# An f32 FFN kernel on one core: a weight's high half moved to VectorE, a small conditioning network moved between convolutions

## The chip, the cores and the metric

One Trainium2 chip, one of its cores. The metric is the time on the device, in microseconds, of one execution of the whole program. The time before is the median of three runs.

## What is computed

`x` is 32 samples of 32 channels by 512 positions. Two layers follow one another, each with a residual. Cut to what matters here:

```
h   = conv1d(x, K=9, 4 groups) + (cond_128 @ c_weight.T)[:, :, None] + bias
h2  = relu(h @ up_w)**2 @ down_w
h3  = ((h @ fc1_w) @ expert_w) * (sum of the top two of h @ gate_w) @ fc2_w
x   = x + layernorm(h2 + h3)

a   = gelu(cond_128 @ W0 + b0); a = gelu(a @ W1 + b1)
att = softmax(a @ W2 + b2)                 # 32 samples x 8 kernels
agg_w = einsum('bk,koi->boi', att, weight); agg_b = att @ bias_k
y   = agg_w @ x + agg_b                    # a 32x32 mixing of channels, per sample
x   = x + y @ W.T + b + (attention over eight low-rank adapters of y)
```

The "conditioning network" of the title is the lines for `a`, `att`, `agg_w` and `agg_b`. It needs only `cond_128` and weights, and its results are first read by the mixing of the second layer.

## The kernel before, in words

The order of the work on every engine is written out by hand: one function per engine, with semaphores between them. Each engine takes its instructions strictly as they are written, so an instruction that waits holds up everything behind it on that engine.

A tile is four samples (128 rows of X). There are eight tiles, taken in two halves of four (`HALVES`, `TPH`). Products with f32 weights are made of three f32r products, since each operand is split into a high and a low part (`mm3`, L1212 to L1216: high by high, high by low, low by high). The high part is a cast, the low part a subtraction; ScalarE mostly makes the first, VectorE or GpSimd the second.

**The opening.** TensorE convolves the four tiles of the first half (L1233), turns the expert weight (L1396), makes the context rows (L1428) and adds them to the convolutions (`conv_bias`, L1246, which waits for the context rows `s_rows`). Then it multiplies expert and fc2 weights once for all ("E2", L1430 to L1439), for which fc2 must be split: ScalarE casts the high half (L713, L714, into a part of `dn_lo`), GpSimd then subtracts (L555, L556). VectorE in this stretch makes the context rows in four small steps (L985 to L993), the low half of the turned expert weight (L997), two pieces of the up weight's low half (`split_up`, L864) and the four tiles of the activation's low half (`split_H`, L885). TensorE's first `up` chunk waits for the last of these.

**A half.** For each of eight chunks c of the inner dimension TensorE runs `up(c)` (12 matmuls), ScalarE takes the relu, VectorE squares it, both split it into `R_hi`, `R_lo`, and TensorE runs `down(c)` (12 matmuls) into the four banks D. Behind up(0) it runs `gate_rows` (8 matmuls), behind up(1) `gate_logits` (four transposes of 16 rows), behind up(2) two `latent` chunks, and `routed` behind down(1).

**The conditioning network, before.** In the first half TensorE's loop calls `conditioning(c)` (L1459 and following) behind down(2) to down(6): first layer (L1464), second layer (L1467), logits (L1470), transposition of the attention weights (`turn_att`, L1443) and `mixing` (bias L1451, weights L1456). ScalarE takes `hidden` (gelu, L738) and `exp_att` (L743) in c = 5 to 7, VectorE `att_scores` and `att_weights` (L1019 to L1031) in c = 7. The second half begins with VectorE's `split_attT`, `copy_aggb` and `turn_agg` (L1040 to L1051).

**Between the halves.** TensorE runs the four convolutions of the second half back to back (`conv(4)` to `conv(7)`, 24 passes each), then down(7) of the first half, then up(8), the first up chunk of the second half. Per tile VectorE adds the context (`add_ctx`, L874), ScalarE casts (`split_H`, L667), VectorE subtracts (`split_H`, L890). up(8) waits for all four. Then VectorE takes `norm_stats` and `norm_apply` of the first half's tiles (L948 to L965) between the steps of up(8) and up(9).

The matrix banks are D (4), U (2) and M (2). A convolution of the second half writes U[0], U[1], M[0], M[1] in turn (`conv_bank`). The name `fc` in rows of the trace is the buffer `fc2`; once fc2 is split, `cond` is laid over it and holds the network's weights and small results. The buffer shown as `attT` is `attT3` or `attT2`, `tf` a staging buffer, `dn_lo` also fc2's halves, `ex_lo` also the turned expert weight.

```
            for h in range(HALVES):
                if h:
                    conv(TPH)
                    for t in range(1, TPH):
                        conv(TPH + t)
                    down(IC - 1)
```

Of the kernel before, what the change touches and what calls it, by code (L numbers as in the profile page):

```python
# [12 lines left out]
P = 128  # L13
# [3 lines left out]
def bass_adaln_ffn(  # L17
# [89 lines left out]
    with ExitStack() as ctx:  # L107
# [10 lines left out]
        QK = [(U[0], U[1]), (M[0], M[1])]  # L118
        wc_bank = (M[1], U[1], D[1])
# [103 lines left out]
        h1, h2 = cond[:, 288:288 + N], cond[:, 320:320 + N]  # L223
# [406 lines left out]
        def _(act):  # L630
# [82 lines left out]
            act.wait_ge(ld_fc2, 16)  # L713
            nc.scalar.activation(fc2_hi, fc2[:], ACT.Copy).then_inc(s_fc2h, 1)  # L714
# [20 lines left out]
            def hidden(i):  # L735

                act.wait_ge((s_c1p, s_c2p)[i], 1)
                nc.scalar.activation((h1, h2)[i], M[0][:, 0:N], ACT.Gelu, bias=(b0, b1)[i])\  # L738
                    .then_inc((s_c1, s_c2)[i], 1)
# [10 lines left out]
            def copy_attT():  # L750
                act.wait_ge(s_aTp, 1)
                nc.scalar.activation(attT3[:], M[0][0:96, 0:N], ACT.Copy).then_inc(s_aT, 1)
                nc.scalar.activation(attT2[:], M[0][0:KE, 0:N], ACT.Copy).then_inc(s_aT, 1)

            for h in range(HALVES):
                i0 = h * IC
                if h:
                    for t in range(TPH):
                        split_H(TPH + t)
# [22 lines left out]
                for c in range(3, IC):  # L782
                    if h == 0:
                        split_dn(c)
                        if c in (5, 6):
                            hidden(c - 5)
                        if c == 7:
                            exp_att()
# [7 lines left out]
                    if h == 0 and c == IC - 1:  # L796
                        copy_attT()
# [54 lines left out]
        def _(dve):  # L852
# [129 lines left out]

            dve.wait_ge(ld_fs, 16)
# [33 lines left out]
            def att_scores():  # L1017
                dve.wait_ge(s_lgp, 1)
                nc.vector.tensor_tensor(att[:, 0, :], M[0][0:N, 0:KE], b2, ALU.add).then_inc(s_att, 1)  # L1019
# [18 lines left out]
            def split_attT():  # L1038
                dve.wait_ge(s_aT, 1)
                nc.vector.tensor_tensor(attT3[64:96], M[0][64:96, 0:N], attT3[64:96].bitcast(F32),  # L1040
                                        ALU.subtract).then_inc(s_aTl, 1)

            def copy_aggb():
                dve.wait_ge(s_aggbp, 1)
                nc.vector.tensor_copy(aggb[:], U[1][0:N, 0:C]).then_inc(s_aggb, 1)

            def turn_agg():

                dve.wait_ge(s_AGp, 1)
                for b in range(2):  # L1050
                    nc.vector.transpose(agg[:, b * (C // 2):(b + 1) * (C // 2), :].rearrange("i o n -> i (o n)"),  # L1051
                                        M[b][0:C, :]).then_inc(s_agg, 1)

            for h in range(HALVES):
                i0 = h * IC
                if h:
                    split_attT()
                    copy_aggb()
                    turn_agg()
                    for T in range(TPH, TILES):  # L1060
                        add_ctx(T)
                        split_H(T)
                    norm_stats(0)
                    norm_stats(1)
                    norm_apply(0)
# [15 lines left out]
                if h:  # L1081
                    norm_apply(2)
# [10 lines left out]
                for c in range(3, IC):  # L1093
                    if h == 0 and c == 7:
                        att_scores()
                        att_weights()
# [114 lines left out]
        def _(pe):  # L1211
# [6 lines left out]
            def conv(T, samples=range(SPT)):  # L1218
# [42 lines left out]
            def gate_logits(h):  # L1261

                pe.wait_ge(s_gTs, h + 1)
                if h:
                    pe.wait_ge(s_tf, TPH)
# [5 lines left out]
            def up(i):  # L1271
# [4 lines left out]
                if c < 2:  # L1276
                    pe.wait_ge(s_H, TPH * (h + 1))
                    if h:
                        pe.wait_ge(s_tf, c + 1)
# [21 lines left out]
            def down(i):  # L1301
# [5 lines left out]
                for t in range(TPH):  # L1307
                    if h and c == 0:
                        pe.wait_ge(s_x1, t + 1)
                    if h == 0 and c == 0:  # L1310
# [129 lines left out]

            def turn_att():
                pe.wait_ge(s_att, 5)
                nc.tensor.transpose(M[0][0:96, 0:N], att3[:].rearrange("n b k -> n (b k)"), ident[0:N, 0:N])\  # L1443
                    .then_inc(s_aTp, 1)

            def mixing():

                pe.wait_ge(s_aT, 2)
                pe.wait_ge(s_aTl, 1)
                pe.wait_ge(s_R, IC)  # L1450
                nc.tensor.matmul(U[1][0:N, 0:C], attT2[:], bk[:],  # L1451
                                 start=True, stop=True).then_inc(s_aggbp, 1)
                pe.wait_ge(s_wk, 1)
# [109 lines left out]
```

## Time and profile before

| | |
|---|---|
| median of 3 runs | 217.27 us (217.12 to 217.29) |
| the profiled execution, its own time | 217.51 us |
| its span in the trace | 215.7 us |
| TensorE busy | 211.2 us, 98% of the span |
| VectorE busy | 124.8 us, 58% |
| ScalarE busy | 80.1 us, 37% |
| GpSimd busy | 61.8 us, 29% |
| granted TensorE clock | 1.0 of full speed in all slices |

The span is what the trace covers; 1.8 us of the execution's time lie around it. A busy share says how long an engine had an instruction in it, not that the work was dense. The chain of waits follows the work that ended last back to its start, and gives for each matmul the time until the next one could go, so an instruction that makes its neighbour late shows there as a longer piece.

### The profile page before, as it was taken

The numbers are of one execution on the slowest core, as the hardware profiler recorded it, in microseconds if no ns is written. First come the engines' busy times: TensorE is split into PE (matmuls) and PEld (weight loads), VectorE is DVE, ScalarE is ACT, GpSimd is POOL, SyncE is SP. The second block draws the span as 40 slices with busy tenths as digits, with TensorE's granted clock in tenths as the row PEclk, the third lists the DMA queues.
The fourth block names the chain that finished last, engine by engine and source line by source line (L and its number), as shares of the span: only waits on it lengthen the run. The fifth ranks groups of instructions, "written<-read, shape, count | busy, mean of one in ns | idle before, by whom it ended". The sixth has DMA issues, their size and how long they took to land.

```text
span 215.7 us, 3106 instructions
## 1 busy us (share of the span) xinstructions
PE 211.2 (98%) x1155; PEld 183.4 (85%) x1155; DVE 124.8 (58%) x265; ACT 80.1 (37%) x156; POOL 61.8 (29%) x77
## 2 busy tenths in 40 slices
PE   7999899999999999999999999999999999999994
PEld 7997778888887789987888888888998998999984
DVE  4979356869525455597852034456996537435443
ACT  5998555369384612222222034431013112121110
POOL 3018421340475620021960012442264202202000
PEclk9999999999999999999999999999999999999999
DMA  6999655310000000174645000000000110110104
GB/s 177 346 406 406 219 116 109 61 27 0 0 3 0 0 0 3 25 123 68 91 41 146 0 0 0 3 0 2 0 3 0 49 49 3 50 49 0 52 0 146
DMA packets 31455, 14.94 MB, mean 69 GB/s; under 512 B 25336, under 2 KB 26168, under 8 KB 31440
## 3 DMA queue, kind: packets, MB, share of 16 engines
q1 hardware_dynamic: 30624, 14.05, 23.4%
q10 hardware_dynamic: 816, 0.69, 1.5%
q8 instruction: 9, 0.15, 0.3%
q14 instruction: 6, 0.05, 0.1%
HBM read 12.62 MB, written 2.11 MB: 68 GB/s over the span
## 4 chain that ended last, share of the span: by engine, by line
PE 95%; DVE 4%; issue 0%; DVEq 0%
PE PS L1214 26%; PE PS L1216 25%; PE PS L1215 25%; PE PS L1233 9%; PE PS L1341 3%; PE PS L1403 2%; DVE up_lo L864 1%; DVE H_lo L885 1%; PE PS L1258 1%; PE PS L1257 1%; PE PS L1412 1%; PE PS L1370 0%; PE PS L1267 0%; DVE ex_lo L997 0%; DVE up_hi L993 0%; PE PS L1456 0%
## 5 line engine op out<-in xcount | busy, mean ns | idle before, releaser
L910 DVE TENSOR_TENSOR PS<-PS,relu 128x512 f32<-128x512 f32 x16 | 11.2, 699 | 30.9 <-ACT relu L675 30.9
L1214 PE MATMUL PS<-H_hi,up_hi 128*128 128x512 f32 x64 | 25.6, 399 | 0.5 <-DVE H_lo L885 0.5
L1216 PE MATMUL PS<-H_hi,up_lo 128*128 128x512 f32 x64 | 25.0, 390 | 0.0
L1215 PE MATMUL PS<-H_lo,up_hi 128*128 128x512 f32 x64 | 25.0, 390 | 0.0
L1233 PE MATMUL PS<-wconv,XS 128*128 128x128 f32 x192 | 22.4, 276 | 0.0
L1233 PEld LDWEIGHTS PS<-wconv,XS 128*128 128x128 f32 x192 | 21.9, 192 | 0.3
L1216 PE MATMUL PS<-qkT_hi,H_lo 128*128 128x320 f32 x64 | 19.8, 309 | 0.0
L1215 PE MATMUL PS<-qkT_lo,H_hi 128*128 128x320 f32 x64 | 19.8, 309 | 0.0
L1214 PE MATMUL PS<-qkT_hi,H_hi 128*128 128x320 f32 x64 | 19.7, 308 | 0.0
L675 ACT ACTIVATE relu<-PS 128x512 f32<-128x512 f32 x16 | 9.5, 594 | 25.5 <-PE PS L1216 23.0
L595 POOL TENSOR_TENSOR X<-X,rowb 128x512 f32<-128x512 f32 x8 | 10.3, 1297 | 28.1 <-PE PS L1341 28.1
L1214 PE MATMUL PS<-dn_hi,ring 128*128 128x512 f32 x44 | 17.4, 396 | 0.0
L1216 PE MATMUL PS<-dn_hi,ring 128*128 128x512 f32 x44 | 17.2, 390 | 0.0
L1215 PE MATMUL PS<-dn_lo,ring 128*128 128x512 f32 x44 | 17.1, 389 | 0.0
L567 POOL TENSOR_TENSOR dn_lo<-dn_raw,dn_hi 128x512 fp32r<-128x512 f32 x8 | 10.3, 1291 | 22.2 <-ACT dn_hi L655 22.2
L449 ACT ACTIVATE XS<-X 32x128 f32<-32x128 f32 (+2 forms) x24 | 15.8, 658 | 0.4
L448 DVE COPY XS<-X 32x128 f32<-32x128 f32 (+2 forms) x40 | 15.2, 380 | 0.7
L1214 PEld LDWEIGHTS PS<-H_hi,up_hi 128*128 128x128 f32 x64 | 12.0, 188 | 3.4 <-issue 0.9
L1216 PEld LDWEIGHTS PS<-H_hi,up_lo 128*128 128x128 f32 x64 | 12.0, 188 | 2.6
L1215 PEld LDWEIGHTS PS<-H_lo,up_hi 128*128 128x128 f32 x64 | 12.0, 188 | 2.3
L1214 PE MATMUL PS<-wT_hi,H_hi 128*128 128x512 f32 (+1 forms) x36 | 13.7, 381 | 0.0
L1216 PE MATMUL PS<-wT_hi,H_lo 128*128 128x512 f32 (+1 forms) x36 | 13.2, 367 | 0.0
(187 smaller groups left out, 459.6 us busy)
## 6 DMA issues: line engine op xcount, KB each, us to landing
up_raw<-in_L_ffn_up_w_dram SPq DMA_DIRECT2D x2, 1024.0 KB, 8.9
dn_raw<-in_L_ffn_down_w_dram SPq DMA_DIRECT2D x2, 1024.0 KB, 13.0
out_dram<-X SPq DMA_DIRECT2D x7, 256.0 KB, 2.0
X<-in_x_dram SPq DMA_DIRECT2D x1, 1024.0 KB, 13.9
XS<-in_L_ffn_W_dram SPq DMA_DIRECT2D x16, 64.0 KB, 2.3
X<-in_x_dram SPq DMA_DIRECT2D x2, 256.0 KB, 2.9
X<-in_x_dram SPq DMA_DIRECT2D x1, 512.0 KB, 5.4
fc<-in_L_ffn_fc_w_dram SPq DMA_DIRECT2D x1, 512.0 KB, 5.7
```

Of the source, the lines that this page charges most:

```text
L448: return nc.vector.tensor_copy(dst, src)
L449: return nc.scalar.activation(dst, src, ACT.Copy)
L567: nc.gpsimd.tensor_tensor(dn_lo[:, c, :], dn_raw[:, c, :], dn_hi[:, c, :].bitcast(F32), ALU.subtract).then_inc(s_dn, 1)
L595: nc.gpsimd.tensor_tensor(X[:, T, :], X[:, T, :], rowb[:], ALU.add).then_inc(s_x1b, 1)
L675: nc.scalar.activation(relu[:], U[i % 2], ACT.Relu).then_inc(s_relu, 1)
L910: nc.vector.tensor_tensor(U[i % 2], U[i % 2], relu[:], ALU.mult).then_inc(s_sq, 1)
L1214: nc.tensor.matmul(o, lh, rh, start=start, stop=False)
L1215: nc.tensor.matmul(o, lh, rl, start=False, stop=False)
L1216: return nc.tensor.matmul(o, ll, rh, start=False, stop=stop)
L1233: last = nc.tensor.matmul(conv_bank(T)[:, s * P:(s + 1) * P], XS[:, T % TPH * SPT + s, a:a + P], wconv[:, a], start=(a == 0 and (T >= TPH ...
L1341: last = nc.tensor.matmul(mix_bank(T)[:, p, :], X[:, T, p * P:(p + 1) * P], BD[:, T], start=True, stop=True)
L1403: nc.tensor.matmul(D[0][:, 0:w], ones[:], ones[:, 0:w], start=True, stop=True)
```

## The change

- **Opening.** The cast of fc2's high half leaves ScalarE. VectorE makes it behind `cT` and `cwT` and ahead of the context rows.
- **The network's matrix steps** leave the first half's loop. The first layer goes ahead of conv(4), the second behind it, the logits behind conv(5), the transposition behind conv(7). Three of them now take or give full 128-column operands (`h2_wide`, `att3_wide`, `ident[:]`).
- **Mixing** goes behind up(8), and its bias product, now `mixing_bias`, behind the second half's `gate_logits`. Banks change accordingly (`agg_bank` is M[1], U[1]; logits M[1]; transposition U[0]; bias D[0]).
- **ScalarE** takes gelu, gelu, exp and the two small copies in turn ahead of the four casts of the second half's tiles. **VectorE** takes the softmax steps behind tile 5, `split_attT` ahead of tile 7's subtraction, `turn_agg` between `norm_stats(1)` and `norm_apply(0)`, `copy_aggb` behind the ninth chunk's split.
- Waits follow: conv(6) waits for the second gelu, conv(7) for the first softmax step, up(9) for both halves of `turn_agg`, up(8) for the turned weights beside the tiles; gate_logits of the second half waits for one half of `turn_agg`.

```diff
@@ scalar @@
             for i in range(3):
                 shift_copies(i)
-            act.wait_ge(ld_fc2, 16)
-            nc.scalar.activation(fc2_hi, fc2[:], ACT.Copy).then_inc(s_fc2h, 1)
             act.wait_ge(s_exTp, 1)
...
                 if h:
-                    for t in range(TPH):
-                        split_H(TPH + t)
+                    hidden(0)
+                    split_H(TPH)
+                    hidden(1)
+                    split_H(TPH + 1)
+                    exp_att()
+                    split_H(TPH + 2)
+                    copy_attT()
+                    split_H(TPH + 3)
                 up_relu(i0)
@@ vector @@
             nc.vector.tensor_copy(cwT[:], M[0][:, N:N + C]).then_inc(s_cT, 1)
 
+            dve.wait_ge(ld_fc2, 16)
+            nc.vector.tensor_copy(fc2_hi, fc2[:]).then_inc(s_fc2h, 1)
             dve.wait_ge(ld_fs, 16)
...
                 if h:
-                    split_attT()
-                    copy_aggb()
-                    turn_agg()
                     for T in range(TPH, TILES):
                         add_ctx(T)
+                        if T == TILES - 1:
+                            split_attT()
                         split_H(T)
+                        if T == TPH + 1:
+                            att_scores()
+                            att_weights()
                     norm_stats(0)
                     norm_stats(1)
+                    turn_agg()
                     norm_apply(0)
...
                 up_split(i0 + 1)
                 if h:
+                    copy_aggb()
                     norm_apply(2)
@@ tensor @@
                 if T == TPH:
                     pe.wait_ge(s_R, IC)
-                if T == TPH + 1:
-                    pe.wait_ge(s_aggb, 1)
                 if T == TPH + 2:
-                    pe.wait_ge(s_lat, LC)
-                    pe.wait_ge(s_agg, 2)
+                    pe.wait_ge(s_c2, 1)
+                if T == TPH + 3:
+                    pe.wait_ge(s_att, 1)
...
+                    if h and c == 0:
+                        pe.wait_ge(s_tf, 1)
+                        pe.wait_ge(s_aT, 2)
+                        pe.wait_ge(s_aTl, 1)
+                    elif h:
+                        pe.wait_ge(s_agg, 2)
...
+            def cond_logits():
+                pe.wait_ge(s_c2, 1)
+                nc.tensor.matmul(M[1][:, 0:KE], h2_wide, W2, start=True, stop=True).then_inc(s_lgp, 1)
+
             def turn_att():
                 pe.wait_ge(s_att, 5)
-                nc.tensor.transpose(M[0][0:96, 0:N], att3[:].rearrange("n b k -> n (b k)"), ident[0:N, 0:N])\
-                    .then_inc(s_aTp, 1)
+                pe.wait_ge(s_tf, 1)
+                nc.tensor.transpose(U[0][:, 0:P], att3_wide, ident[:]).then_inc(s_aTp, 1)
...
                 if h:
+                    cond_layer0()
                     conv(TPH)
-                    for t in range(1, TPH):
-                        conv(TPH + t)
+                    cond_layer1()
+                    conv(TPH + 1)
+                    cond_logits()
+                    conv(TPH + 2)
+                    conv(TPH + 3)
+                    turn_att()
                     down(IC - 1)
 
                 up(h * IC)
+                if h:
+                    mixing()
                 gate_rows(h)
                 up(h * IC + 1)
                 gate_logits(h)
+                if h:
+                    mixing_bias()
                 up(h * IC + 2)
```

TensorE where the halves meet, before: bias and weights of the mixing, then all 48 convolution matmuls, in one piece.

```order
L1216 MATMUL PS<-dn_hi,ring 128x512
L1451 MATMUL PS<-bk,attT 32x32
L1456 MATMUL PS<-lat_hi,attT 32x512 x2
L1233 MATMUL PS<-wconv,XS 128x128 x48
L1214 MATMUL PS<-dn_hi,ring 128x512
```

And with the change (L1451 is now the first layer, L1455 the second, L1459 the logits, L1464 the transposition):

```order
L1219 MATMUL PS<-dn_hi,ring 128x512
L1451 MATMUL PS<-cT,fc 128x32
L1235 MATMUL PS<-wconv,XS 128x128 x12
L1455 MATMUL PS<-fc 128x32
L1235 MATMUL PS<-wconv,XS 128x128 x12
L1459 MATMUL PS<-fc 128x8
L1235 MATMUL PS<-wconv,XS 128x128 x24
L1464 MATMUL PS<-ident,fc 128x128
```

The convolutions are cut in three places, and the mixing has left this stretch for the one behind up(8).

VectorE in the opening, with the change. The row L984 is new; the rows around it stand in the order that they had.

```order
L981 COPY cwT<-PS 128x32
L984 CAST dn_lo<-fc 128x1024
L987 TENSOR_TENSOR rows<-PS,fsb 64x32
L989 CAST rows_hl<-rows 64x32
L991 TENSOR_TENSOR rows_hl<-rows,rows_hl 32x32
L995 TENSOR_TENSOR up_hi<-rows_hl,turn 64x512
L999 TENSOR_TENSOR ex_lo<-PS,ex_lo 128x512
L864 TENSOR_TENSOR up_lo<-up_raw,up_hi 128x512 x2
L885 TENSOR_TENSOR H_lo<-PS,H_hi 128x4x128 x4
```

The cast now stands ahead of the four small steps of the context rows, which `conv_bias` waits for.

VectorE between the halves, with the change, from tile 5's subtraction to tile 7's:

```order
L890 TENSOR_TENSOR H_lo<-tf,H_hi 128x4x128
L1021 TENSOR_TENSOR fc<-PS,fc 32x8
L1023 TENSOR_REDUCE fc<-fc 32x1
L1025 TENSOR_SCALAR fc<-fc 32x8
L1030 RECIPROCAL fc<-fc 32x1
L1033 TENSOR_SCALAR fc<-fc 32x3x8
L874 TENSOR_TENSOR tf<-PS,B 128x4x4x32
L890 TENSOR_TENSOR H_lo<-tf,H_hi 128x4x128
L874 TENSOR_TENSOR tf<-PS,B 128x4x4x32
L1042 TENSOR_TENSOR attT<-PS,attT 32x32
L890 TENSOR_TENSOR H_lo<-tf,H_hi 128x4x128
```

Five softmax steps and one subtraction are new between the tiles' steps.

## Rows read from the trace of the kernel before

**Rows 1.** The page's chain that ended last, by engine.

```profile
PE 95%; DVE 4%; issue 0%; DVEq 0%
```

**Rows 2.** Waits of TensorE in total, times, longest (us).

```profile
PE PS L1214 <- DVE H_lo L885: 0.5, 1, 0.5
```

**Rows 3.** Chain in order of time, opening: start us, us, what.

```profile
14.82 0.16 PE PS L1428 x2
...
15.50 0.19 DVE rows_hl L989
...
15.71 0.68 DVE up_hi L993
...
17.08 2.71 DVE up_lo L864 x2
19.79 2.41 DVE H_lo L885 x4
...
22.33 0.47 PE PS L1214
```

**Rows 4.** Line L864: duration ns min/median/max, first and last start.

```profile
L864 DVE TENSOR_TENSOR up_lo<-up_raw,up_hi x8: 680/682/2185, 17.0 to 57.6; 128x512 fp32r<-128x512 f32 x8
```

**Rows 5.** Timeline, opening, three engines: start us, us, engine, line, what [idle before].

```profile
13.60 0.18 DVE L981 COPY cwT<-PS 128x32 f32<-128x32 f32 x1
...
14.81 1.06 ACT L714 ACTIVATE dn_lo<-fc 128x1024 fp32r<-128x1024 f32 x1
...
16.02 2.62 POOL L556 TENSOR_TENSOR dn_lo<-fc,dn_lo 128x1024 fp32r<-128x1024 f32 x1 [2.08 <-ACT dn_lo L714]
...
23.45 2.40 POOL L563 TENSOR_TENSOR fc_lo<-fc_raw,fc_hi 128x1024 fp32r<-128x1024 f32 x1 [2.45 <-ACT fc_hi L731]
...
17.48 1.19 PE L1246 MATMUL PS<-up_hi,ones_r 128*128 128x512 f32 x4
```

**Rows 6.** Groups of VectorE by form: busy us, mean ns | idle before.

```profile
L448 DVE COPY XS<-X 32x512 f32<-32x512 f32 x10 | 6.1, 607 | 0.1
...
L1036 DVE TENSOR_TENSOR lat_hi<-tf,lat_hi 32x1024 fp32r<-32x1024 f32 x1 | 1.2, 1215 | 0.2 <-ACT lat_hi L748 0.2
```

**Rows 7.** Chain in order of time, TensorE in the first half's loop.

```profile
57.66 0.14 PE PS L1464 x2
57.80 0.31 PE PS L1214
...
69.08 0.16 PE PS L1470 x2
69.24 0.43 PE PS L1214
```

**Rows 8.** Chain in order of time, TensorE where the halves meet.

```profile
78.02 0.17 PE PS L1451 x2
78.19 0.59 PE PS L1456 x2
78.78 10.72 PE PS L1233 x96
```

**Rows 9.** Timeline between the halves, VectorE and ScalarE.

```profile
81.50 0.69 DVE L874 TENSOR_TENSOR tf<-PS,B 128x512 f32<-128x512 f32 x1 [1.38 <-PE PS L1233]
...
90.92 0.69 DVE L890 TENSOR_TENSOR H_lo<-tf,H_hi 128x512 fp32r<-128x512 f32 x1 [0.70 <-ACT H_hi L667]
...
72.22 1.28 ACT L743 ACT_TABLE_LOAD   x1
```

**Rows 10.** Timeline and chain, up(8) to up(10): VectorE, then TensorE.

```profile
78.82 1.30 DVE L1051 STREAM_TRANSPOSE qk_raw<-PS 32x512 f32<-32x512 f32 x2 [0.41 <-PE PS L1456]
...
97.87 0.68 DVE L914 TENSOR_TENSOR ring_last<-PS,ring_last 128x512 fp32r<-128x512 f32 x1
...
99.52 0.35 PE PS L1267 x4
99.86 0.43 PE PS L1214
```

More of the change, by code:

```diff
@@ L118, in bass_adaln_ffn @@
         QK = [(U[0], U[1]), (M[0], M[1])]
+        agg_bank = (M[1], U[1])
         wc_bank = (M[1], U[1], D[1])
@@ L222, in bass_adaln_ffn @@
         b0, b1, b2 = cond[:, 264:265], cond[:, 265:266], cond[0:N, 266:266 + KE]
-        h1, h2 = cond[:, 288:288 + N], cond[:, 320:320 + N]
+        h1, h2, h2_wide = cond[:, 288:288 + N], cond[:, 0:N], cond[:, 0:P]
+        att3_wide = cond[:, 384:384 + P]
         att = cond[0:N, 352:352 + 4 * KE].rearrange("n (a k) -> n a k", k=KE)
@@ L737, in hidden @@
                 act.wait_ge((s_c1p, s_c2p)[i], 1)
-                nc.scalar.activation((h1, h2)[i], M[0][:, 0:N], ACT.Gelu, bias=(b0, b1)[i])\
+                nc.scalar.activation((h1, h2)[i], M[0][:, i * N:(i + 1) * N], ACT.Gelu, bias=(b0, b1)[i])\
                     .then_inc((s_c1, s_c2)[i], 1)
@@ L795, in _ @@
                         split_wk()
-                    if h == 0 and c == IC - 1:
-                        copy_attT()
                     for g in groups_after(h, c):
@@ L1264, in gate_logits @@
                 if h:
-                    pe.wait_ge(s_tf, TPH)
+                    pe.wait_ge(s_agg, 1)
                 for t in range(TPH):
@@ L1309, in down @@
                         pe.wait_ge(s_x1, t + 1)
+                        pe.wait_ge(s_aggb, 1)
                     if h == 0 and c == 0:
@@ L1439, in _, with cond_layer0, cond_layer1 @@
                 last.then_inc(s_E2p, 1)
+            def cond_layer0():
+                pe.wait_ge(ld_cond, 16 * 7)
+                pe.wait_ge(s_lat, LC)
+                nc.tensor.matmul(M[0][:, 0:N], W0, cT[:, 0], start=True, stop=True).then_inc(s_c1p, 1)
+            def cond_layer1():
+                pe.wait_ge(s_c1, 1)
+                nc.tensor.matmul(M[0][:, N:2 * N], W1, h1, start=True, stop=True).then_inc(s_c2p, 1)
+            def cond_logits():
+                pe.wait_ge(s_c2, 1)
+                nc.tensor.matmul(M[1][:, 0:KE], h2_wide, W2, start=True, stop=True).then_inc(s_lgp, 1)
@@ L1453, in mixing, with mixing_bias @@
                 pe.wait_ge(s_wk, 1)
+                pe.wait_ge(s_tf, TPH)
                 wf = wk3.rearrange("k o i -> k (o i)")
                 for b in range(2):
-                    last = nc.tensor.matmul(M[b][0:N, :], attT3[:], wf[:, b * BANK:(b + 1) * BANK],
+                    last = nc.tensor.matmul(agg_bank[b][0:N, :], attT3[:], wf[:, b * BANK:(b + 1) * BANK],
                                             start=True, stop=True)
                 last.then_inc(s_AGp, 1)
-            def conditioning(c):
-                if c == 2:
-                    pe.wait_ge(ld_cond, 16 * 7)
-                    nc.tensor.matmul(M[0][:, 0:N], W0, cT[:, 0], start=True, stop=True).then_inc(s_c1p, 1)
-                elif c == 3:
-                    pe.wait_ge(s_c1, 1)
-                    nc.tensor.matmul(M[0][:, 0:N], W1, h1, start=True, stop=True).then_inc(s_c2p, 1)
-                elif c == 4:
-                    pe.wait_ge(s_c2, 1)
-                    nc.tensor.matmul(M[0][0:N, 0:KE], h2, W2, start=True, stop=True).then_inc(s_lgp, 1)
-                elif c == 5:
-                    turn_att()
-                elif c == 6:
-                    mixing()
+            def mixing_bias():
+                pe.wait_ge(s_x1, 1)
+                nc.tensor.matmul(D[0][0:N, 0:C], attT2[:], bk[:], start=True, stop=True).then_inc(s_aggbp, 1)
@@ L1493, in _ @@
                         routed(h)
-                    if h == 0:
-                        conditioning(c)
                     if c + 3 < IC:
```

26 lines of the change are left out of this document (6 added, 20 removed).

## The prediction

> **What bounds the kernel now.** I read the chain of waits first. TensorE is on it for 95% of the span and VectorE for 4% [rows 1]. So a step taken from ScalarE, or moved on VectorE, is worth something only where TensorE waits for it. Second come TensorE's own waits: apart from its start it waits once, 0.5 us, in its first `up` chunk, for VectorE's last `H_lo` [rows 2]. Third, the chain around that wait [rows 3]: four small VectorE steps follow the context matmul (two are shown, at 15.50 and 15.71), then two `up_lo` pieces, four `H_lo` tiles, and up(0) at 22.33. Fourth, the same chain in the first half's loop: each step of the conditioning network lies on it, and so costs TensorE time directly [rows 7, 8]. There are thus two places to cost: at most 0.55 us in the opening, and what the network's small matmuls cost where they stand against where they go.
>
> **The opening.** Now: ScalarE casts fc2's high half from 14.81 to 15.87, and GpSimd's subtraction (L556) runs from 16.02 to 18.64 [rows 5]. The telling row is `up_lo`: eight of a kind, 0.68 us in the median, one of 2.185 [rows 4]. The long one is the first, begun at 17.0, and it ends at about 19.2, some 0.55 us after GpSimd's end. I read this as VectorE being held until GpSimd's subtraction was done: 2.185 - 0.68 = 1.50 us lost. The subtraction's own 2.62 us against 2.40 for its like (L563) [rows 5] fit the reverse: it came while L993 (15.71 to 16.39, [rows 3]) was running. Both `up_lo` and L993 read two SBUF operands; L997 between them reads one from PSUM.
>
> With the change the cast runs on VectorE from 13.78, behind L981 [rows 5], while VectorE is idle until the context matmul ends at 14.98 [rows 3]. The trace has no such cast. Its bounds: a 512-element copy is 0.607 us, and a 1024-element subtraction 1.215 us [rows 6]. I take the middle, 0.91: the copy is the nearer in kind, but has half the elements. The Trainium skill ("VectorE: DVE Perf Modes", The perf-mode tier table) gives an f32 copy within SBUF two elements a cycle, 1227 ns for 2048; an estimate from that page is 0.7 us here, which would make the opening 0.2 us shorter than the sum below. No row here shows it.
>
> GpSimd then starts 0.15 us behind the cast, as now, at 14.84, and ends 2.40 later, at 17.24. But now it is in flight when L989 (at 15.50) and L993 come up, both of two SBUF operands. If they are held as `up_lo` was, L989 ends just behind GpSimd and L993 0.75 behind it, at 17.99 instead of 16.39. `conv_bias`, at 17.48 now [rows 5] and waiting for L993, goes at about 18.1: TensorE gets a gap of 0.6 us there. From L993's end to the last `H_lo` is 22.20 - 16.39 = 5.81 us now; less the 1.50 of holding, which is gone, 4.31. So the last `H_lo` ends at 22.30, and up(0) starts 0.13 later, at 22.43 instead of 22.33: **+0.10 us**. In general up(0) = 21.52 + the cast: -0.20 with 0.61, +0.41 with 1.215. The wait is moved from `up_lo` to the context rows, not removed. The rule is one of the Trainium skill too ("SBUF — State Buffer", Who interferes with whom): VectorE instructions with two SBUF inputs and GpSimd instructions that read SBUF lock each other out for a whole instruction. By that rule the opening gains nothing; without it, 0.55. The trace agrees, with the row of 2.185. What ScalarE gains (1.06 us) is worth nothing: its casts of H wait for `conv_bias`. The weight loads that wait for fc2's split are issued about 1.4 us sooner, and nothing on the chain waits for them.
>
> **The network's matmuls, taken out.** The first layer takes 0.14 and lengthens the next matmul from 0.23 to 0.31: 0.22; the second layer is the same. The logits, of 32 columns of weights, take 0.16 and lengthen the next to 0.43: 0.36; the transposition shows the same two pieces [rows 7]. Bias and weights of the mixing take 0.17 + 0.59 = 0.76, and the convolutions behind them are not lengthened [rows 8]. Sum: 2 x 0.22 + 2 x 0.36 + 0.76 = 1.92 us.
>
> **Put in.** First layer, second layer and logits now stand before convolutions, with full 128-column weights like L1428, which costs 0.16 amid convolutions [rows 3]; I take 0.16 for each, and for the transposition, which also is full now: 0.64. The mixing costs 0.59 as before, plus between 0 and 0.20 for the lengthened neighbour (0.43 - 0.23): 0.69. The bias, 0.17 plus the same doubt: 0.27. Sum 1.60, between 1.40 and 1.80. Net **-0.32 us** (-0.52 to -0.12).
>
> **The waits that are added.** They cost nothing as long as the following cover holds.
> (a) conv(5) to up(8). A tile's convolution is 10.72 / 4 = 2.68 us [rows 8]; `add_ctx` starts 2.72 behind the convolution's start, and the tile's `H_lo` ends 2.07 behind that (91.61 against 81.50 + 3 x 2.68) [rows 8, 9]. Count from `add_ctx(5)`: `H_lo(5)` ends at 2.07; three softmax steps of about 0.2 (an estimate from L989's 0.19, [rows 3]) make 2.67. ScalarE's table load for exp, 1.28 us [rows 9], comes ahead of the waiting instruction; it starts behind the cast of tile 5 at 1.37 and is over at 2.65. exp and its readout 0.35 (an estimate, two small pieces), two more steps: 3.4 to 3.5, so `add_ctx(6)` is late by some 0.7, behind VectorE's queue. `H_lo(6)` ends at 5.6, `H_lo(7)` at 7.7. up(8) wants to start at -2.72 + 3 x 2.68 + 2 x 0.16 + 12 x 0.23 = 8.4. It has 0.7 us to spare; before, up(8) stood at 78.78 + 10.72 + 12 x 0.23 = 92.26 and `H_lo(7)` at 91.61, 0.65 to spare. conv(7)'s wait for the first softmax step (2.3 against 2.8) holds by 0.5; both gelus are done a convolution early.
> (b) up(8) to up(10). `turn_agg` (1.30 us, [rows 10]) can't start before the mixing is done, and now stands ahead of `up_square(8)` on VectorE. From 0.15 behind the mixing: 1.30, then `norm_apply`, the square, `norm_stats(2)` and `up_split(8)`, which are five full-width pieces of 0.7 (as L874 and L914, [rows 9, 10]) and a small one of 0.2: 5.15 us in all. up(10) needs that; TensorE meanwhile has 8 x 0.23, 12 x 0.23, 0.55 for `gate_logits` (0.35 and a neighbour of 0.43, [rows 10]) and 0.27: 5.4. There are 0.2 us to spare, where it was 99.86 - 98.55 = 1.3. The bias product is also needed only by down(8), later by far.
>
> **Sum.** +0.10 - 0.32 = -0.22 us. Against the profiled execution's own 217.51 that is 217.29; against the median, 0.24 lower, **217.05 us**. The terms' bounds make -0.72 to +0.29, so 216.55 to 217.55. That is 0.1% down; about 0.2%, 0.43 us, is what a measurement of this kernel can tell from no change.
>
> **Rivals.**
> - *The short steps are not held.* If VectorE's small steps and L993 pass beside GpSimd, `conv_bias` stays at 17.48, `H_lo` is done by 20.7 and up(0) follows the E2 product at 21.78: -0.55 - 0.32, **216.4 us**. For it: L989 reads 32 partitions only, and the trace never shows one like it beside GpSimd. Against it: L993 itself seems to have held GpSimd up by 0.22.
> - *The table load waits* (slower). If ScalarE loads the table for exp only once the softmax's third step is there, it is loaded at 2.67 + 1.28 = 3.95; weights at 4.8, `H_lo(6)` at 6.9, `H_lo(7)` at 8.9, up(8) at 9.05 instead of 8.4: +0.65, **217.7 us**. It decides once `add_ctx(6)` starts later than 4.2, that is once the load ends behind 3.35. For it: the cover is thin. Against it: the load stands as an instruction of its own ahead of the one that waits.
> - *VectorE is late for up(10)* by (b): with a mixing that costs 0.59 only and a step more on VectorE, the 0.2 us turn into a stall of up to 0.3, which gives back the matmuls' gain: **217.35 us**.
>
> **How the numbers follow.** The sum as argued 0.50 (a bit over a quarter of it below 216.84, by a short cast and cheap mixing); steps not held 0.20; late table 0.12; late for up(10) 0.13; several of the bad ends together 0.05. Faster by over 0.2% is 0.20 + 0.14 = 0.34; slower by over 0.2% is most of the late table, a little of the others and the last case, 0.13; within, 0.53. The range takes in the first rival and reaches just over the second: 216.4 to 217.75. The likeliest case's own is 216.55 to 217.55.
>
> **What would show it.** In the opening: no `up_lo` of over 0.7 us before 22, but one long L991 or L995; GpSimd's subtraction from about 14.8; a gap on TensorE before L1246 of about 0.6 us, and up(0) between 22.1 and 22.75. Wrong if `conv_bias` still starts at 17.5. In the first half: down(6) ends about 1.2 us earlier against up(0). Between the halves: pieces of 0.16 for the small matmuls, no TensorE wait before up(8), `add_ctx(6)` late by 0.7 behind the softmax, the table load inside ScalarE's wait. Behind up(8): mixing of 0.6 to 0.8, no wait of up(10). A TensorE wait in any of these places names the failing step.

## The result and the profile after

| | before | after |
|---|---|---|
| median of 4 runs each | 217.25 us (217.12 to 217.29) | 219.5 us (219.3 to 219.78) |
| ratio, 95% interval | | 1.0105 (1.0088 to 1.0123) |
| profiled execution, its span | 217.51, 215.7 us | 219.3, 217.4 us |
| start of up(0) | 22.33 us | 24.66 us |
| from there to the end of the span | 193.37 us | 192.74 us |

The kernel became 1.0% slower; 217.05 us had been predicted, within 216.4 to 217.75. The last two rows split the result: up(0) starts 2.33 us later, and what follows it is 0.63 us shorter (193.37 - 192.74; the spans are given to 0.1). The forecast was +0.10 and -0.32. The two profiled executions differ by 1.79 us and not by the medians' 2.25: that of before is a little longer than its median, that of after the shortest of its four. In the sets below some executions (27 of 80 of before, three of six of e2, two of ten of e8, one of eight of e11; none of them was traced) lie over 1.5% above the fastest of their kernel, and the ratios leave those out.

The waits of TensorE look harmless (waited for: us in total, times, longest; compare [rows 2]):

```profile
PE PS L1410 <- DVE ones L968: 1.1, 1, 1.1
PE PS L1248 <- issue: 0.6, 1, 0.6
PE PS L1217 <- DVE H_lo L885: 0.3, 1, 0.3
```

The first row is the wait for the first operand at the start. The first of the two behind it is the gap of 0.6 us that was forecast, and the second was 0.5 before. The chain in order of time shows why they mislead (compare [rows 3]; start us, us, what):

```profile
6.04 7.77 PE PS L1235 x48
...
17.18 0.20 DVE rows L987
...
17.40 2.00 DVE rows_hl L989
...
19.63 0.68 DVE up_hi L995
...
20.92 1.20 DVE up_lo L864 x2
22.12 2.41 DVE H_lo L885 x4
...
24.66 0.47 PE PS L1217
```

There are two new things. The first 48 convolution passes take 7.77 us, where they took 5.68 before (the chain there: `6.02 5.68 PE PS L1233 x48` in its first 14 us). And L989, a cast of 64 x 32 elements, takes 2.00. It is L987 in the kernel before, where the timeline has it at 0.17:

```profile
15.29 0.17 DVE L987 CAST rows_hl<-rows 64x32 fp32r<-64x32 f32 x1
```

The timeline after, VectorE and then GpSimd:

```profile
13.78 0.69 DVE L984 CAST dn_lo<-fc 128x1024 fp32r<-128x1024 f32 x1
...
17.40 1.99 DVE L989 CAST rows_hl<-rows 64x32 fp32r<-64x32 f32 x1
...
14.62 2.36 POOL L558 TENSOR_TENSOR dn_lo<-fc,dn_lo 128x1024 fp32r<-128x1024 f32 x1 [0.72 <-DVE dn_lo L984]
16.93 0.51 POOL L559 MEMSET gate_hl<- 128x512 uint32 x1
17.39 0.94 POOL L560 MEMSET tf<- 96x1024 f32 x1
18.28 0.17 POOL L562 MEMSET fc<- 32x96 f32 x1
18.40 0.94 POOL L563 MEMSET BD<- 128x1024 f32 x1
```

The subtraction is over at 16.98, before L989 is even issued. But four memsets follow it without a gap, the last ends at 18.40 + 0.94 = 19.34, and the cast ends at 19.39. Before, the same cast came while GpSimd was idle (its subtraction started at 16.02).

TensorE where the halves meet and behind it, by the chain (compare [rows 8, 10]):

```profile
79.05 0.14 PE PS L1451 x2
79.19 2.76 PE PS L1235 x24
81.95 0.14 PE PS L1455 x2
82.09 2.76 PE PS L1235 x24
84.85 0.12 PE PS L1459 x2
84.98 5.46 PE PS L1235 x48
90.44 0.11 PE PS L1464
...
96.02 0.47 PE PS L1472 x2
...
101.39 0.17 PE PS L1478 x2
101.57 0.43 PE PS L1217
```

No TensorE wait stands here. The covers that were thin, in the timeline:

```profile
88.23 0.66 DVE L874 TENSOR_TENSOR tf<-PS,B 128x512 f32<-128x512 f32 x1
...
91.86 0.69 DVE L890 TENSOR_TENSOR H_lo<-tf,H_hi 128x512 fp32r<-128x512 f32 x1 [0.48 <-ACT H_hi L669]
...
100.58 0.68 DVE L914 TENSOR_TENSOR ring_last<-PS,ring_last 128x512 fp32r<-128x512 f32 x1
...
86.26 1.28 ACT L743 ACT_TABLE_LOAD   x1
```

The table load runs at 86.26, straight behind the cast of tile 5, ahead of the instruction that waits: the late table did not come.

### The profile page after: what moved, and what is told of

It reads as the page before. It is cut to its first block, busy times and chain, and to the rows that moved or that the text cites. A ratio compares the mean times of both kernels' runs of the same rounds, so it can differ in the third digit from the quotient of the medians.

```text
span 217.4 us, 3111 instructions
## 1 busy us (share of the span) xinstructions
PE 212.7 (98%) x1155; PEld 186.0 (86%) x1155; DVE 125.3 (58%) x266; ACT 79.6 (37%) x155; POOL 61.6 (28%) x77
## 4 chain that ended last, share of the span: by engine, by line
PE 95%; DVE 4%; issue 0%; DVEq 0%
PE PS L1217 26%; PE PS L1219 25%; PE PS L1218 25%; PE PS L1235 10%; PE PS L1348 3%; PE PS L1410 2%; DVE H_lo L885 1%; DVE rows_hl L989 1%; PE PS L1260 1%; PE PS L1259 1%; PE PS L1419 1%; DVE up_lo L864 1%; PE PS L1377 0%; PE PS L1269 0%; DVE up_hi L995 0%; DVE ex_lo L999 0%
## 5 line engine op out<-in xcount | busy, mean ns | idle before, releaser
L1235 PE MATMUL PS<-wconv,XS 128*128 128x128 f32 x192 | 25.0, 293 | 0.0
L1235 PEld LDWEIGHTS PS<-wconv,XS 128*128 128x128 f32 x192 | 24.1, 208 | 0.1
L450 DVE COPY XS<-X 32x128 f32<-32x128 f32 (+2 forms) x40 | 15.1, 378 | 0.7
```

What stands on the lines that cost most here:

```text
L450: return nc.vector.tensor_copy(dst, src)
L1235: last = nc.tensor.matmul(conv_bank(T)[:, s * P:(s + 1) * P], XS[:, T % TPH * SPT + s, a:a + P], wconv[:, a], start=(a == 0 and (T >= TPH ...
```

## The experiments

**The theories.** The *hold*: VectorE's small cast is kept out until GpSimd's unbroken queue, memsets included, is through. The *clock*: TensorE's slower first 4 us push everything back, and the long cast is only a symptom. Of the second, the rows, before and then after, for the convolution passes from 6 to 10 us (durations ns min/median/max):

```profile
L1233 PEld LDWEIGHTS PS<-wconv,XS x36: 186/192/192, 5.9 to 10.0; 128*128 128x128 f32 x36
```

```profile
L1235 PEld LDWEIGHTS PS<-wconv,XS x20: 286/333/333, 6.0 to 10.0; 128*128 128x128 f32 x20
```

And the busy time of each engine from 6 to 8 us, before and after (TensorE and its number of matmuls, then PEld, DVE, ACT, POOL, PEclk, the share of the DMA engines and GB/s; PEld are the weight loads, PEclk is the granted clock):

```profile
6.00:8.00 2.00, 2.00 (x19) 2.00 (x18) 1.87 (x8) 1.94 (x5) 0.00 (x0) 1.00 0.89 303
```

```profile
6.00:8.00 2.00, 2.00 (x10) 2.00 (x10) 1.87 (x8) 1.94 (x5) 0.00 (x0) 1.00 0.93 260
```

Half as many matmuls in the same time, loads of 333 ns where they took 192, and a granted clock of 1.00 in both. I read the slow stretch as the lower level (1.2 GHz of 2.4) and the column as not showing it before the clock's first rise; later in an execution the column does show the lower level (e11 below). From 10.9 us on, the loads are 192 ns after too. TensorE did the same 14 warming and 12 turning matmuls ahead of it in both.

### The parts alone

`e1_cast_only`: before, with the cast of fc2's high half on VectorE and nothing else.

```diff
-            act.wait_ge(ld_fc2, 16)
-            nc.scalar.activation(fc2_hi, fc2[:], ACT.Copy).then_inc(s_fc2h, 1)
...
+            dve.wait_ge(ld_fc2, 16)
+            nc.vector.tensor_copy(fc2_hi, fc2[:]).then_inc(s_fc2h, 1)
```

> The kernel before, with the cast of fc2's high half on VectorE and nothing else changed. Theory A (the late rise of TensorE's clock in the opening, 2.1 us of convolutions at half speed, comes with the network's new place or with the program as a whole, not with the cast): convolutions begin at full speed at about 6.0 us; the cast takes 0.69 us, the context rows wait for GpSimd, up(0) starts 22.2 to 22.6, and the time is 217.1 to 217.5. Theory B (the cast brings the late rise): first 48 convolution passes take 7.8 us instead of 5.7, up(0) near 24.7, and the time is 219.3 to 219.6.

Measured: 220.32 us, 1.0153 (1.0125 to 1.018). up(0) starts at 25.08, and 193.42 us follow, as before the change. The small cast (L987 there) takes 2.74 us, from 17.07 to 19.80; GpSimd's last memset ends at 18.82 + 0.94 = 19.76. The first 48 passes take 7.45 us, so this run has both new things, and does not say which of them costs the time.

`e2_network_only`: the change without that cast (the diff above reversed in the changed kernel).

> The changed kernel with the cast back on ScalarE where it was, so only the network's move is left. Theory A (clock rise late by the program as a whole): either state of the opening is possible; if it starts at full speed, the move alone gives 0.5 to 0.6 us, 216.7; if at half speed, 218.8. Theory C (the move itself costs the 2 us through waits between the halves): 219 or more with an opening as before, up(0) at 22.3. Theory B: 216.7.

Measured: 216.44 us, 0.9965 (0.9948 to 0.9981), from the three runs at 216.29 to 216.5; the other three took 220.5. The profile has 192.73 us behind up(0), and 193.37 was the time before: the 0.64 us are the network's. It starts up(0) at 21.77, 0.56 earlier than before, because the warming and the turning of the conv weights took 3.20 + 0.90 us instead of 3.35 + 1.47 and the passes began at 5.28. No step that e2 moves stands ahead of up(0), so this part of that execution's gain is not put down to the change. `up_lo` is held again (2.78 for two). So the loss comes with the cast alone, and the network's part shortens what stands behind up(0).

### The clock against the hold

`e3_after_warm10` and `e4_before_warm10`: six more warming matmuls (20 for 14, as `warm` makes two at a time) at each kernel's start, so that TensorE has worked longer when the convolutions begin.

```diff
-            warm(7)
+            warm(10)
```

> The changed kernel with ten warm-up matmuls on TensorE ahead of the opening instead of seven (0.7 us more of them, ahead of work that waits for its load anyway in part). Theory A: the clock is up when the convolutions begin, or rises early in them; the time falls from 219.5 to between 216.9 and 217.8. If the late rise were due to anything behind the warm-up (loads, ports), it stays at 219.5 or adds the 0.7 us.

Measured: 219.36 us, 1.0101 (1.0083 to 1.0119). The 48 passes take 5.70 us now, so the clock is up, and the context matmul is done 1.0 us sooner. It changes nothing:

```profile
18.62 0.94 POOL L563 MEMSET BD<- 128x1024 f32 x1
...
16.43 3.16 DVE L989 CAST rows_hl<-rows 64x32 fp32r<-64x32 f32 x1
```

The cast starts 0.97 us earlier and takes 1.17 us longer, to 19.59, 0.03 behind the memset's 19.56. The late clock is thus not the cause of this loss.

> The kernel before with ten warm-up matmuls instead of seven. Its clock was up at 5.9 us already. Theory A says no gain: 217.3 to 218.0, as up to 0.7 us of warm-up may push the turning of the convolution weights back. It is the control for the run before.

Measured: 217.8 us, 1.0025 (1.001 to 1.0041), up(0) at 22.42. Its passes take 5.70 us, as they did without the six. With the clock up in both, after is still 1.56 us slower.

### What holds the cast

`e5_no_small_cast`: in the changed kernel the cast reads PSUM and SBUF instead of copying the sum from SBUF: the same value is computed once more.

```diff
-            nc.vector.tensor_copy(rows_hl[:], rows[:]).then_inc(s_ctx, 1)
+            nc.vector.tensor_tensor(rows_hl[:], M[0][0:2 * N, 64:64 + C], fsb[:], ALU.add).then_inc(s_ctx, 1)
```

> The changed kernel, with the small cast of the context rows' high part (64x32, SBUF to SBUF) replaced by a tensor_tensor that adds PSUM and fsb again and writes the high part itself; it then reads one SBUF operand, like the step ahead of it. Theory P (the small cast alone is held for GpSimd's whole queue: subtraction and four memsets; steps with two SBUF operands are held only by the subtraction): the step takes 0.2 us, the next one (two SBUF operands) ends with GpSimd's subtraction at about 17.0, conv_bias starts near 17.9 with the clock up early, up(0) at 22.2 to 22.5, and the time is 216.4 to 216.9. Theory Q (any step on VectorE that touches SBUF is held as long as GpSimd is busy): the next step is held for 3 us instead, and the time stays at 219.3.

Measured: 216.98 us, 0.9976 (0.9952 to 1.0001), up(0) at 22.29.

```profile
14.82 2.36 POOL L558 TENSOR_TENSOR dn_lo<-fc,dn_lo 128x1024 fp32r<-128x1024 f32 x1 [0.72 <-DVE dn_lo L984]
17.11 0.54 POOL L559 MEMSET gate_hl<- 128x512 uint32 x1
...
15.06 0.18 DVE L989 TENSOR_TENSOR rows_hl<-PS,fsb 64x32 fp32r<-64x32 f32 x1
15.28 1.95 DVE L991 TENSOR_TENSOR rows_hl<-rows,rows_hl 32x32 fp32r<-32x32 f32 x1
17.27 0.68 DVE L995 TENSOR_TENSOR up_hi<-rows_hl,turn 64x512 fp32r<-64x512 f32 x1
```

This is the picture that the prediction had drawn: L991, with two SBUF operands, is held until the subtraction is over (14.82 + 2.36 = 17.18) and no longer, and L995 passes beside the memsets at its usual 0.68. L989, with one operand in PSUM, passes beside the subtraction. So memsets hold this cast from SBUF to SBUF, and don't hold the two-operand instruction beside them. The median lies just above the 216.4 to 216.9 that was expected.

`e6_memsets_behind_rows`: the cast stays, GpSimd waits for the context rows between its subtraction and its memsets.

```diff
             nc.gpsimd.tensor_tensor(fc2_lo, fc2[:], fc2_hi.bitcast(F32), ALU.subtract).then_inc(s_fc2, 1)
+            pool.wait_ge(s_rows, 1)
             nc.gpsimd.memset(gate_hl[:].bitcast(mybir.dt.uint32), 0).then_inc(s_gatez, 1)
```

> The changed kernel, with GpSimd's memsets behind its subtraction held back until the context rows are written. Theory P: the small cast now ends with the subtraction at 17.0 instead of 19.4 to 19.6, so up(0) is at 22.4 to 22.6 with the clock up early; 216.5 to 217.0. Theory R (it is not the memsets that hold the cast but, say, the weight loads or the late clock): no change, 219.3. The loads of the network's weights and wk wait for one of these memsets and come up to 2 us later, which nothing feels.

Measured: 217.16 us, 0.998 (0.9954 to 1.0007), up(0) at 22.59.

```profile
14.93 2.35 POOL L558 TENSOR_TENSOR dn_lo<-fc,dn_lo 128x1024 fp32r<-128x1024 f32 x1 [0.72 <-DVE dn_lo L985]
18.31 0.52 POOL L560 MEMSET gate_hl<- 128x512 uint32 x1 [1.03 <-DVE up_hi L996]
...
14.95 2.36 DVE L990 CAST rows_hl<-rows 64x32 fp32r<-64x32 f32 x1
```

The same cast now ends with the subtraction (17.28). One wait on GpSimd, in an idle place, and up(0) starts 2.07 us earlier than in after. Not all of that is the hold's: this profile, like e5's, also has the clock up early (its 48 passes take 5.79 us by the timeline, those of after 7.84). Behind passes as late as in after the cast could not start before 17.40; at 0.17 it would end at 17.57, 0.26 behind the 17.31 here, so about 0.3 of the 2.07 is the clock's (worked out, not run). The loss itself does not hang on that: all ten runs of e6 lie under 218.0, all four of after at 219.3 or more. The run moves some loads of weights along with the memsets, so it does not rule them out by itself; e10 and e11 below do.

`e7_memsets_first`: three of the memsets go to the front of GpSimd's work, where it is idle.

```diff
+            nc.gpsimd.memset(gate_hl[:].bitcast(mybir.dt.uint32), 0).then_inc(s_gatez, 1)
+            nc.gpsimd.memset(tflat[0:96], 0.0).then_inc(s_wkz, 1)
+            nc.gpsimd.memset(BD[:], 0.0).then_inc(s_zero, 1)
+            pool.wait_ge(s_zero, 3)
             pool.wait_ge(xs_v, 9)
```

> The changed kernel, with the memsets of gate_hl, tf and BD ahead of GpSimd's wait for VectorE's copies of X, at about 3.1 to 5.5 us, where GpSimd sits idle. Theory P for the small cast: it waits for the subtraction only, up(0) at 22.4 to 22.6 if nothing else moves. What is open: whether VectorE's copies of X (L450, SBUF to SBUF) are held by memsets as well. If they are, the first convolutions start late by up to 2 us and the time is 217.5 to 219; if not, 216.5 to 217.0.

Measured: 218.5 us, 1.0036 (1.0005 to 1.0066), up(0) at 23.90. The cast is free of memsets (17.49 to 18.62, the subtraction ends at 18.59), but the subtraction itself comes 1.62 us later than after, since VectorE was held at the other end. Its copies of the shifted input (L450), e7 and then after:

```profile
L450 DVE COPY XS<-X x28: 260/266/1650, 3.9 to 13.7; 32x128 f32<-32x128 f32 x20, 32x256 f32<-32x256 f32 x8
```

```profile
L450 DVE COPY XS<-X x30: 247/266/385, 3.7 to 12.9; 32x128 f32<-32x128 f32 x20, 32x256 f32<-32x256 f32 x10
```

The first copy, of 0.27 elsewhere, takes 1.65 us while the memsets run (3.13 to 5.44): it starts at 3.86 and ends at 5.51. The place was idle on GpSimd, but its memsets there held VectorE.

### The dose

If the memsets hold the cast, one memset more must hold it longer.

`e10_one_more_memset`: BD is cleared twice, so GpSimd's run of memsets is 0.96 longer. Its order needs a wait between the two.

```diff
             nc.gpsimd.memset(BD[:], 0.0).then_inc(s_zero, 1)
+            pool.wait_ge(s_zero, 3)
+            nc.gpsimd.memset(BD[:], 0.0).then_inc(s_zero, 1)
```

> The changed kernel with the memset of BD made twice on GpSimd, one more memset of 0.94 us at the end of the queue behind the subtraction; the output is the same. Theory P: the small cast is held until the last memset is done, 0.95 to 1.0 us longer, so up(0) moves from 24.7 to 25.6 and the time from 219.4 to 220.3. If the cast were held by the subtraction or by the late clock, no change.

Measured: 219.76 us, 1.012 (1.0105 to 1.0134), up(0) at 24.95. The additional memset did not act:

```profile
18.70 0.94 POOL L563 MEMSET BD<- 128x1024 f32 x1
19.70 0.96 POOL L565 MEMSET BD<- 128x1024 f32 x1
...
17.30 2.37 DVE L991 CAST rows_hl<-rows 64x32 fp32r<-64x32 f32 x1
```

The cast ended at 19.67, in the 0.06 us between the two memsets that the wait had opened. That made the theory sharper: not all of GpSimd's work counts, only what follows without a gap. No load waits for a memset of BD, and yet the cast gets in right behind one.

`e11_memset_no_gap`: a memset of 0.96 us of a buffer not yet in use, straight behind the subtraction, with no wait.

```diff
             nc.gpsimd.tensor_tensor(fc2_lo, fc2[:], fc2_hi.bitcast(F32), ALU.subtract).then_inc(s_fc2, 1)
+            nc.gpsimd.memset(ring_last[:].bitcast(mybir.dt.uint32), 0)
```

> The changed kernel with one more memset on GpSimd (the still unused ring_last, 0.94 us) between its subtraction and the memset of gate_hl, with no wait between, so that the queue stays without a gap; the output is the same. The run with a second memset of BD had a semaphore wait ahead of it, and the small cast got in at just that gap. Theory P, so amended (a two-port cast gets in only where GpSimd has a gap): the cast is held until the last memset is done, 0.9 us longer than in the change, up(0) at 25.5 to 25.9, time 220.2 to 220.5. If any finished GpSimd instruction let it in, nothing changes: 219.4.

Measured: 220.88 us (218.24 to 221.71), 1.0143 (1.0105 to 1.0181).

```profile
19.51 0.94 POOL L564 MEMSET BD<- 128x1024 f32 x1
...
14.87 5.62 DVE L990 CAST rows_hl<-rows 64x32 fp32r<-64x32 f32 x1
...
21.52 1.80 PE L1249 MATMUL PS<-up_hi,ones_r 128*128 128x512 f32 x4 [4.22 <-issue]
```

A cast of 2048 elements lasts 5.62 us, through the subtraction and five memsets, to 20.49 (GpSimd: 20.45). The cast ended 1.1 us later than in after, where 0.9 was expected; the memset was 0.96 and GpSimd began 0.23 later. The DMA engines stay as busy behind it as before it (share 1.05 or 1.06 from 19 to 24 us), so it was not the loads that ended the hold. The time came out above the 220.2 to 220.5 expected, because TensorE idles 4.2 us in front of `conv_bias` and its clock then falls: the granted clock is 1.00 up to 21 us, 0.91 from 21 to 22, and 0.50, the lower level, from 22 to 25; the four `conv_bias` matmuls take 1.80 instead of 1.18.

The end of GpSimd's unbroken run gives the cast's end in all seven kernels where it falls beside a busy GpSimd, and up(0) with it:

| kernel | last of the run ends | cast ends | up(0) | up(0) less the run's end |
|---|---|---|---|---|
| after | 19.34 | 19.39 | 24.66 | 5.32 |
| e1 | 19.76 | 19.80 | 25.08 | 5.32 |
| e3 | 19.56 | 19.59 | 24.87 | 5.31 |
| e6 (subtraction alone) | 17.28 | 17.31 | 22.59 | 5.31 |
| e7 (subtraction alone) | 18.59 | 18.62 | 23.90 | 5.31 |
| e10 | 19.64 | 19.67 | 24.95 | 5.31 |
| e11 | 20.45 | 20.49 | (clock fell) | |

### Building on it

`e8_network_narrow`: e2 with the logits and the transposition in their narrow form of before.

```diff
-                nc.tensor.matmul(M[1][:, 0:KE], h2_wide, W2, start=True, stop=True).then_inc(s_lgp, 1)
+                nc.tensor.matmul(M[1][0:N, 0:KE], h2, W2, start=True, stop=True).then_inc(s_lgp, 1)
...
-                nc.tensor.transpose(U[0][:, 0:P], att3_wide, ident[:]).then_inc(s_aTp, 1)
+                nc.tensor.transpose(U[0][0:96, 0:N], att3[:].rearrange("n b k -> n (b k)"), ident[0:N, 0:N]).then_inc(s_aTp, 1)
```

> The network's move alone (cast on ScalarE), with logits and transposition in their narrow forms as before the change (32 rows out, 96x32). The prediction took the full-width forms as 0.2 us cheaper each. If so this is 0.2 to 0.5 us slower than the move alone with wide forms, about 216.8 against 216.4; if width does not matter, the same 216.4.

Measured: 217.01 us, 0.998 (0.9958 to 1.0002), from eight runs, with two more at 220.9; 193.07 us behind up(0), against e2's 192.73. The chain of e8:

```profile
82.32 0.16 PE PS L1459 x2
82.48 5.56 PE PS L1235 x48
88.04 0.16 PE PS L1464
88.20 0.43 PE PS L1217
```

After has 0.12, 5.46 and 0.11 in the rows above, and 0.23 for the matmul that follows. The wide form is worth 0.34 us by the spans: about half of the network's gain is not in where the steps stand but in their width. (The medians, 217.01 and 216.44, differ by more, as up(0) also starts 0.36 us later in e8's profile than in e2's.)

`e9_split_on_vector`: e5, with fc2's subtraction on VectorE too, right behind the cast.

```diff
             nc.vector.tensor_copy(fc2_hi, fc2[:]).then_inc(s_fc2h, 1)
+            dve.wait_ge(s_fc2h, 1)
+            nc.vector.tensor_tensor(fc2_lo, fc2[:], fc2_hi.bitcast(F32), ALU.subtract).then_inc(s_fc2, 1)
```

> The changed kernel without the small cast (as in the run of that name) and with the subtraction of fc2's low half on VectorE behind the big cast; GpSimd only waits for it and then does its memsets. Theory P: no step is held in the opening. Cast 0.7 and subtraction 1.2 us end at about 15.7 to 15.9, the context rows are written by 17.2, conv_bias is not late, up_lo takes 0.68 each, and up(0) follows the E2 product without a wait, 0.5 us earlier than without the small cast: 216.3 to 216.6. If holding were not by GpSimd's instructions but by something else in the opening, the steps stay long and it is 217 or more.

Measured: median 216.37 us, seven runs at 215.95 to 216.47 and five at 217.27 to 217.89; 0.9979 (0.9957 to 1.0). up(0) at 21.54.

```profile
14.73 1.23 DVE L985 TENSOR_TENSOR dn_lo<-fc,dn_lo 128x1024 fp32r<-128x1024 f32 x1
...
16.51 0.68 DVE L996 TENSOR_TENSOR up_hi<-rows_hl,turn 64x512 fp32r<-64x512 f32 x1
```

VectorE takes 1.23 us for what GpSimd takes 2.36 for, and no step is long any more; up(0) comes 0.75 us sooner than in e5.

`e12_best`: e9, with the second piece of `up_lo` behind the four `H_lo`.

```diff
             split_up(0)
-            split_up(1)
             split_H(0)
...
             split_H(3)
+            split_up(1)
```

> The version with the whole fc2 split on VectorE and without the small cast, and with the second up_lo piece on VectorE behind the four H_lo tiles instead of ahead of them. The last 0.3 us that TensorE waits in up(0) should go, since the last H_lo ends 0.6 us sooner: up(0) at 21.2 with the clock up early, 0.3 us less than that version, 215.7 to 216.2. If the wait only moves to up(1), no gain.

Measured: median 216.95 us, six runs at 215.7 to 216.42 and six at 217.48 to 218.11; 0.9982 (0.9949 to 1.0016). Its profile shows one of the longer runs: TensorE's only wait is that at its start, yet up(0) starts at 22.99, since the first 48 passes took 7.38 us. Here, with VectorE no longer in the way, the late clock is the bound; by the passes' times, 7.38 - 5.68, it is worth up to 1.7 us there (worked out, not run). Its shorter six runs lie about where the expectation had them (215.7 to 216.2), the longer six do not. Whether e12 is faster than before is not settled. Of all versions only e2, the network's part alone, has an interval that lies wholly below 1, and it rests on three runs of six.

## Why the prediction was wrong, point by point

- **The failing step** is this one of the opening: "now it is in flight when L989 (at 15.50) and L993 come up, both of two SBUF operands. If they are held as `up_lo` was, L989 ends just behind GpSimd". It counted as exposed only steps with two SBUF operands, and as holding only the subtraction. (Line numbers are those of before: its L989 is the 32 x 32 subtraction, L991 in the changed kernel.) The cast one row ahead of them (L987; L989 in the changed kernel), of one operand, was taken as free, at the 0.17 us that it had shown beside an idle GpSimd; and the four memsets were not looked at. The cast is held, and through all of them: 19.34 instead of 17.24 for the end of GpSimd's hold, +2.10, which with 0.13 of smaller steps (L991 behind the cast, 0.2; the stretch from L995 to up(0), 0.1 shorter than worked out) is the whole difference between up(0) at 22.43 and at 24.66. Without the cast (e5) up(0) starts at 22.29, where the prediction had it. No row of before showed a cast from SBUF beside a busy GpSimd, and the text should have listed it with bounds. The Trainium skill has it ("SBUF — State Buffer", Who interferes with whom): casts can take the shared pair of ports, and the later of the two engines is blocked for the whole instruction. The traces agree (e6: the cast lasts 2.36 us, to 0.03 behind the subtraction) and go further: back-to-back instructions of GpSimd act as one (e11, 5.62 us), and a gap of 0.06 us ends the hold (e10).
- **fc2's cast**: 0.69 us, where the sum took 0.91 between 0.61 and 1.215. The estimate of 0.7 from the Trainium skill ("VectorE: DVE Perf Modes", The perf-mode tier table) was the nearer. GpSimd's subtraction took 2.36 and began at 14.62, against 2.40 and 14.84, so it ended at 16.98 instead of 17.24. None of this enters the loss, as the cast behind it was held past both.
- **The gap on TensorE before `conv_bias`** came out at 0.6 us, as predicted, and proves nothing: `conv_bias` starts at 20.42 instead of 18.1. TensorE reached it some 2.1 us late too, with its lower clock. A wait shows the difference of two delays; only the start times show the loss. That the number fits is luck. The prediction's test "up(0) between 22.1 and 22.75" was the one that told.
- **The clock** in the first 4 us of convolutions was not in the prediction. It cost nothing in after, because the cast would have been held to the same time (e3), and it is the next bound once nothing is held (e12).
- **The network's matmuls**: right mechanism, size off: the gain came out at twice the forecast. Put in, the four small steps take 0.14 + 0.14 + 0.12 + 0.11 = 0.51 (0.64 forecast), but the convolutions behind them 10.98 instead of 10.72, +0.26, which the sum had as none; the mixing 0.47 (0.69), the bias 0.17 (0.27). Together 1.41, where 1.60 was forecast. Taken out, the steps inside the first half were worth 1.30 us and not 1.16: from up(0) to where the halves meet it is 78.02 - 22.33 = 55.69 before (and 80.77 - 25.08 in e1), and 79.05 - 24.66 = 54.39 after. The chain of before shows where the 0.14 probably hid: behind a small step not only the next matmul is longer, but one or more of the next few read 0.24 instead of 0.23, too little to see in one row. With both, the forecast of -0.32 becomes -0.32 - 0.19 - 0.14 = -0.65; measured are -0.63 (after) and -0.64 (e2).
- **The added waits**: as worked out. `add_ctx(6)` starts at 88.23, behind the softmax; the last `H_lo` ends at 92.55 with up(8) at 93.3, about 0.7 to spare; VectorE's split for up(10) ends at 101.26, 0.3 ahead of 101.57 (0.2 forecast). Neither the late table nor the late up(10) came. The first rival, steps not held, is refuted by L991 in e5 (1.95 us beside the subtraction).
- **Range and rivals**: the slower rival stood in the network and came to 217.7, 0.4 us above before. The real loss was in the opening and brought the median 2.25 above before, five times as much, so the upper bound of 217.75 held nothing of it.

## What to carry to other kernels

Before an instruction is moved into another engine's time, list every instruction of both engines in the overlap, the small ones too, and ask of each which operands lie in SBUF; the price of a hold is the rest of the other engine's unbroken queue, not the size of the instruction held. An SBUF-to-SBUF copy or cast on VectorE beside GpSimd's memsets is the case to look for: give it an operand in PSUM (e5), put a wait into GpSimd's queue behind what must be early (e6), or do both halves of the split on VectorE (e9, which has e5's form of the small cast too). And read the start time of the stage behind, as the longest wait can stay the same while two delays grow together.

## What the runs showed of the hardware that was not expected

- VectorE's cast of 64 x 32 elements lasted 0.17 us beside an idle GpSimd, and 1.13 (e7), 2.00 (after), 2.36 (e6), 2.37 (e10), 2.74 (e1), 3.16 (e3) and 5.62 (e11) beside busy ones, always ending 0.03 to 0.05 us behind the end of GpSimd's unbroken run. A two-operand instruction from SBUF was held by the subtraction only (e5), and not by memsets.
- TensorE's clock reached its upper level at different moments in kernels whose first 6 us are the same work: the passes took 5.68 us in before and 7.77 in after, 7.45 in e1, 5.86 in e2 (begun at 5.28), 7.38 in e12's profile. The granted clock reads 1.00 in the slow stretch too; only the load durations, 333 ns against 192, and the number of matmuls in a stretch show it. Six more warming matmuls brought 5.70 in the changed kernel and left before, early without them, at 5.70. Of the nine profiles with the big cast on VectorE and no more warming, five have the late clock (after, e1, e7, e10, e12) and four the early one (e5, e6, e9, e11); the three with that cast on ScalarE (before, e2, e8) have the early one. The cast itself runs only at about 14 us, behind those passes, and what decides the moment is not settled.
- The two small matmuls with operands of 32 columns or rows cost more than the same with full 128, in themselves (0.16 us each against 0.11 to 0.12) and in what stands behind them (e8 against after: 48 convolution passes of 5.56 us against 5.46, and one matmul of 0.43 against 0.23).
